# Unpacked expert weights, and their cast on GpSimd instead of ScalarE, in the last stage of a four-part transformer kernel

## The chip, the cores and the metric

The kernel runs on one core of a Trainium2 chip. The metric is the device time of one execution in microseconds. A core has the engines TensorE (PE), VectorE (DVE), ScalarE (ACT), GpSimd (POOL) and SyncE (SP), and 16 DMA engines that all queues share.

## The reference

x has 4 x 1024 tokens of 256 numbers. Four parts follow one another, each added to x after a layer norm:

```python
x = x + _L0_attn_ref(_layernorm(x), ...)   # a gated recurrence over the sequence
x = x + _L0_ffn_ref(_layernorm(x), ...)    # 8 experts, the 2 best of each token
x = x + _L1_attn_ref(_layernorm(x), ...)   # causal attention, 16 heads of 64
x = x + _L1_ffn_ref(_layernorm(x), ...)    # 32 experts, the 4 best of each token
```

The last part is the one that the change touches. D is 256, I is 128, E is 32, K is 4, and an expert takes at most C = 256 tokens. The expert weights W1, W3 (32 x 256 x 128) and W2 (32 x 128 x 256) are bfloat16:

```python
scores = jax.nn.sigmoid((X @ gate_w.T).astype(jnp.float32))
_, idx = jax.lax.top_k(scores + bias[None, :], K)
...
xe = jnp.zeros((E, C, D), x.dtype).at[eid, posc].add(jnp.where(valid[:, None], Xrep, ...))
h = jax.nn.silu(jnp.einsum('ecd,edi->eci', xe, W1)) * jnp.einsum('ecd,edi->eci', xe, W3)
ye = jnp.einsum('eci,eid->ecd', h, W2)
...
out = yrows.reshape(-1, K, D).sum(axis=1)
out = out + jax.nn.silu(X @ sw1.T) * (X @ sw3.T) @ sw2.T
```

## The kernel before

Each engine has its own program, in one block, and they meet through semaphores. Four stages stand one after another with a barrier between them (finish_stage). The first three (recurrence, first experts, attention) end at about 2093 us.

The fourth stage first finishes the routing of the last tokens and computes the shared expert for 8 groups of 512 tokens. POOL scatters each token's normalised row, with its token number and its gates, to the places that its experts have in the HBM tensor routed1 (scatter_rows, L856). Rows of it are 289 numbers, 1156 B.

Then come the 32 routed experts. For one expert e, which uses the slot q = e mod 8 (EBUF is 8) of each buffer:

- SP loads its 256 rows into d_xe (load_rows, L739) and its packed weights, 128 partitions x 768 bfloat16 numbers, into d_wb (load_weights, L733). The first eight experts' weights are loaded at the start of the stage, all others when VectorE and the casting engine are done with the slot (s_dec2, s_dec), after the rows of the same expert.
- A cast makes 32-bit numbers of them in d_wf. ScalarE casts W1 and W3 (128 x 512, cast_weights, L1254), four experts ahead; VectorE casts W2 (128 x 256, L1920).
- TensorE transposes the rows (transpose_rows, L2472) and ScalarE and VectorE split them in a high and a low part (L1227, L1904). VectorE also copies token numbers and gates out (d_tok, d_gate, L1902 and L1903), for which the slot's previous scatter must have landed.
- TensorE multiplies by W1 and W3 (hidden, L2485). ScalarE's tanh (L1231) and VectorE (L1912, L1914) make the gated hidden layer d_eh, which is again split (L1236, and L1924 for d_eh_lo).
- TensorE multiplies by W2 (second_layer, L2496), ScalarE scales by the gates into d_y (take_y, L1246). d_y has 4 slots (YBUF), so this waits until the rows of the expert four before have landed.
- POOL adds the 2 x 128 rows into one of two accumulators in HBM, acc[0] for even and acc[1] for odd experts, with an indirect DMA that adds (add_rows, L923). It waits for the tile of d_y and for the previous adds to the same accumulator.

TensorE runs hidden(e), transpose_rows(e + 2), second_layer(e - 2) in turn. When all adds have landed, SP loads both accumulators, 8 groups of 512 tokens each (L761), VectorE adds them (L1948), and ScalarE's queue stores the result (L1293). In these loads and stores, partition p has 4 neighbouring tokens of a group, 4096 B in one run.

Of the kernel before, what the change touches and what calls it, by code (L numbers as in the profile page):

```python
# [11 lines left out]
ACT = mybir.ActivationFunctionType  # L12
AX_X = mybir.AxisListType.X

P = 128
# [27 lines left out]
        self.eng.wait_ge(self.sem, at if self.i is None else self.i * self.per + at)  # L43


def network(nc, x_in, a_params, w12T, w3T, gate0T, wqkT, wvT, woT, swT, bias1, ewT, out):
    B, S, D = x_in.shape
    T = B * S
    NT = T // P
    KD = D // P  # L50
# [2 lines left out]
    K0 = 2  # L53
    NH, DQ = wqkT.shape[2], wqkT.shape[3] // 2
    N = (a_params.shape[1] - 3 * D - 4 - 2 * KD) // (4 * KD)
    E1, I1 = bias1.shape[0], ewT.shape[1]
    K1 = 4
    C1 = 2 * (2 * 512) * K1 // E1
    G = 4
    GT = G * P  # L60
    NG = T // GT
# [9 lines left out]
    Z_SCALE = (DQ / D) ** 0.5 * (D / DQ) ** 0.5 / NH  # L71

    x_tiles = x_in.rearrange("b (i p) d -> p (b i) d", p=P)
    out_rows = out.rearrange("b s d -> (b s) d")
    TOK, GATE = D, D + 1
    FIRST, GAP, SECOND = D + 1, D + 2, D + 3
    routed0 = nc.dram_tensor("routed0", (E0 * REGION, D + 4), F32).ap()
# [5 lines left out]
    routed1 = nc.dram_tensor("routed1", (E1 * C1, W_ROW), F32).ap()  # L83
# [3 lines left out]
    with ExitStack() as ctx:  # L87
# [42 lines left out]
        X = place("X", [P, NT, D])  # L130
# [164 lines left out]
        EBUF = 8  # L295
# [270 lines left out]
        def _(sp):  # L566
# [162 lines left out]
            def load_weights(e, q):  # L729

                sp.wait_ge(s_dec, e + 1)
                sp.wait_ge(s_dec2, e + 1)
                sp.dma_start(d_wb[:, q, :], ewT[bass.ds(e, 1), :, :].rearrange("e p d -> p (e d)")).then_inc(s_dw[q], 16)  # L733

            def load_rows(e, q):

                sp.wait_ge(s_det, e + 1)
                sp.wait_ge(s_dgt, e * 2 + 2)
                sp.dma_start(d_xe[:, q, :, :], routed1[bass.ds(e * C1, C1), :].rearrange("(p a) d -> p a d", p=P)).then_inc(s_dxe[q], 16)  # L739


            for q in range(EBUF):
# [16 lines left out]
            for g in range(NG):  # L759
                for j, rows in enumerate((X, d_acc)):  # L760
                    sp.dma_start(rows[:, g * G:(g + 1) * G, :],  # L761
                                 acc[j][g * GT:(g + 1) * GT, :].rearrange("(p q) d -> p q d", p=P)).then_inc(s_x[g], 16)
            sp.wait_ge(s_out, 16 * NG)

        @block.gpsimd
        def _(pool):
# [50 lines left out]
            def add_rows(n, r):  # L817

                if not (isinstance(n, int) and n == 0):
                    pool.wait_ge(s_bst, n * 16)  # L820
                pool.wait_ge(s_btk, n + 3)
                pool.wait_ge(s_bye, n + 3)
                pool.sem_inc(s_pass, 1)
                pool.indirect_dma_start(acc0, bass.IndirectOffsetOnAxis(ap=b_tok[:, r:r + 1], axis=0),  # L824
                                        b_y[:, r, :], None, compute_op=ALU.add).then_inc(s_bst, 16)
# [84 lines left out]
            for n in range(2):  # L910
                pool.wait_ge(s_dslot, NG - 1 + n)
                scatter_rows(NG - 2 + n, n, range(G * K1))

            def add_rows(e, half, q):

                j = q % 2

                if not (isinstance(half, int) and half == 0):
                    pool.wait_ge(s_dyst[j], half * 32)
                for a in range(C1 // P):  # L920
                    pool.wait_ge(s_dye, e * 2 + (a + 5))
                    pool.sem_inc(s_pass, 1)
                    pool.indirect_dma_start(acc[j], bass.IndirectOffsetOnAxis(ap=d_tok[:, q, a:a + 1], axis=0),  # L923
                                            d_y[:, q % YBUF, a, :], None, compute_op=ALU.add).then_inc(s_dyst[j], 16)

            pool.wait_ge(s_dax, 16 * (NT + 2 * (C1 // P) + NG))
            for q in range(EBUF):
                add_rows(q, q // 2, q)
            with pool.Fori(0, E1 // EBUF - 1) as i:
                for q in range(EBUF):  # L930
                    add_rows(i * EBUF + (q + EBUF), i * (EBUF // 2) + (EBUF // 2 + q // 2), q)

        @block.scalar
        def _(act):
# [311 lines left out]
                    act.activation(d_y[:, q % YBUF, a, :], PS[:, 4 + q % 2, a * D:(a + 1) * D], ACT.Identity,  # L1246
                                   bias=zeros[:, 0:1], scale=d_gate[:, q, a:a + 1]).then_inc(s_dye, 1)

            def cast_weights(e, q, eighth):

                act.wait_ge(s_dw[q], eighth * 16 + 16)

                act.wait_ge(s_deh, e + 1)
                act.activation(d_wf[:, q, 0:2 * D], d_wb[:, q, 0:2 * D], ACT.Copy).then_inc(s_dec, 1)  # L1254

            for c in range(4):
                cast_weights(c, c, 0)
            for j in range(2):
                take_rows(j, j)
            for e in range(2):  # L1260
                tanh_half(e, e)
                take_rows(e + 2, e)
                cast_weights(e + 4, e + 4, 0)
                take_hidden(e, e)

            for r in range(EBUF):
                tanh_half(r + 2, r % 2)
                take_rows(r + 4, r % 2)
                cast_weights(r + 6, (r + 6) % EBUF, (r + 6) // EBUF)
                take_y(r, r // 2, r, r >= YBUF)  # L1270
                take_hidden(r + 2, r % 2)
            with act.Fori(0, E1 // EBUF - 2) as i:
                for r in range(EBUF):
                    e, j = i * EBUF + (EBUF + r + 2), r % 2
                    tanh_half(e, j)
                    take_rows(e + 2, j)
                    cast_weights(e + 4, (r + 6) % EBUF, i + (1 + (r + 6) // EBUF))
                    take_y(e - 2, i * (EBUF // 2) + (EBUF // 2 + r // 2), r)
                    take_hidden(e, j)
            for r in range(EBUF - 2):  # L1280
                e, j = E1 - EBUF + r + 2, r % 2
                tanh_half(e, j)
                if e + 2 < E1:
                    take_rows(e + 2, j)
                if e + 4 < E1:
                    cast_weights(e + 4, (e + 4) % EBUF, E1 // EBUF - 1)
                take_y(e - 2, (e - 2) // 2, r)
                take_hidden(e, j)
            for e in range(E1 - 2, E1):
                take_y(e, e // 2, e % EBUF)  # L1290
            for g in range(NG):
                act.wait_ge(s_x4, g + 1)
                act.dma_start(out_rows[g * GT:(g + 1) * GT, :].rearrange("(p q) d -> p q d", p=P), X[:, g * G:(g + 1) * G, :]).then_inc(s_out, 16)  # L1293

        @block.vector
        def _(dve):
# [610 lines left out]
            def gate_hidden(e, q, eighth, ahead):  # L1907
                j = q % 2
                dve.wait_ge(s_deth, e + 1)

                dve.wait_ge(s_deg, e + 1)
                st.done(dve.scalar_tensor_tensor(d_eh[:, j, :], d_eth[:, j, :], 1.0, PS[:, 2 + j, 0:C1], ALU.add, ALU.mult))  # L1912
                st.sync()
                dve.scalar_tensor_tensor(d_eh[:, j, :], d_eh[:, j, :], 0.5, PS[:, 2 + j, C1:2 * C1], ALU.mult, ALU.mult).then_inc(s_dep, 1)  # L1914
                if ahead:
                    low_rows(e + 2, (q + 2) % EBUF, eighth * (EBUF // 2) + (q + 2) // 2, not isinstance(e, int) or e + 2 >= EBUF)
                dve.wait_ge(s_dw[q], eighth * 16 + 16)

                dve.wait_ge(s_dey, e + 1)
                dve.tensor_copy(d_wf[:, q, 2 * D:3 * D], d_wb[:, q, 2 * D:3 * D]).then_inc(s_dec2, 1)  # L1920
# [652 lines left out]
```

## Time and profile before

| | |
|---|---|
| median of 3 runs | 2332.34 us (2330.44 to 2339.95) |
| the profiled execution | 2332.34 us, of which the span is 2330.6 us |
| mean granted TensorE clock | 0.918 of full speed |
| last stage, first load to end | about 2093 to 2330.6 us |
| scatter-adds of the routed experts | 64, from 2172.34 to 2291.64 us (starts) |

The span is the time from the first to the last recorded instruction. The profile is of one execution. Times inside it are given in microseconds from the start of the span, or in nanoseconds for the mean of one instruction. The rest of the profile is in the section with rows.

### The profile page before, as it was taken

The page shows a single profiled execution, that of the slowest core. Times are in us where ns is not written, and L with a number is a line of the kernel's source. Part 1 is how long each engine was busy: PE and PEld are TensorE (multiplying, and loading weights), DVE is VectorE, ACT ScalarE, POOL GpSimd, SP SyncE. Part 2 cuts the span into 40 slices and gives each one's busy share as a digit, 9 for nine tenths or more (in the row PEclk, how much of TensorE's full clock was granted, in tenths as well). Part 3 has the DMA queues.
Part 4 walks back from the last instruction along what each step waited for, and adds up shares of the span by engine and source line. Part 5 has one row for each costly group of instructions (what it writes and reads, how often), then busy time and mean ns, then how long its engine had stood idle before and what let it go on. Part 6 is the DMA issues. An engine that isn't in the chain of part 4 may idle for free. (4 is left out here: it accounts for less than half of the span.)

```text
span 2330.6 us, 42176 instructions
## 1 busy us (share of the span) xinstructions
PE 2000.4 (86%) x11537; PEld 1412.2 (61%) x11538; DVE 1362.5 (58%) x3643; ACT 1024.4 (44%) x2148; POOL 1144.8 (49%) x1128
## 2 busy tenths in 40 slices
PE   4662999998957999989999989999989999966660
PEld 2352566665635777767777767777767777745550
DVE  7753333332335666665778765777765778648661
ACT  2210333332323555545555544555545555523660
POOL 0055222222210666643667753567753667745583
PEclk8855999999977999999999989999999999987995
DMA  8194222234250111111222111211111111113987
GB/s 309 65 294 166 49 45 45 45 59 131 45 142 18 45 47 46 46 36 33 57 66 55 48 28 32 61 53 48 45 29 42 47 53 47 43 39 126 225 146 244
DMA packets 203593, 186.44 MB, mean 80 GB/s; under 512 B 85418, under 2 KB 184583, under 8 KB 201872
## 3 DMA queue, kind: packets, MB, share of 16 engines
q1 hardware_dynamic: 173168, 149.15, 21.5%
q0 software_dynamic: 29088, 30.89, 8.2%
q10 hardware_dynamic: 1152, 4.19, 0.4%
q8 instruction: 85, 1.39, 0.2%
q14 instruction: 100, 0.82, 0.1%
HBM read 101.74 MB, written 82.95 MB: 79 GB/s over the span
## 5 line engine op out<-in xcount | busy, mean ns | idle before, releaser
L881 POOL TENSOR_TENSOR c_den<-c_den,c_p 128x512 f32<-128x512 f32 (+3 forms) x576 | 550.9, 956 | 359.5 <-ACT c_p L1094 288.5
L1094 ACT ACTIVATE c_p<-PS 128x512 f32<-128x512 f32 (+3 forms) x768 | 350.5, 487 | 348.7 <-PE PS L2178 236.6
L2199 PE MATMUL PS<-c_p,c_vh 128*64 128x256 f32 (+1 forms) x2816 | 336.1, 352 | 0.0
L2147 PE MATMUL PS<-c_k,c_q 128*128 128x512 f32 (+2 forms) x768 | 291.1, 381 | 29.8 <-DVE c_max L1601 20.4
L2170 PE MATMUL PS<-c_q,c_k 128*128 128x512 f32 (+2 forms) x768 | 293.0, 385 | 3.3 <-issue 2.2
L2049 PE MATMUL PS<-b_w12T,b_tT 128*128 x576 | 273.7, 598 | 1.4 <-ACT b_tT L988 0.7
L824 POOL DMA_INDIRECT acc<-b_y,b_tok x72 | 111.1, 1543 | 332.4 <-ACT b_y L1005 303.7
L2199 PEld LDWEIGHTS PS<-c_p,c_vh 128*64 128x64 f32 x2816 | 198.4, 137 | 107.0 <-issue 53.6
L2171 PE MATMUL PS<-c_q,c_k 128*128 128x512 f32 (+2 forms) x768 | 259.1, 348 | 0.0
L1085 ACT ACTIVATE c_q<-PS 64x512 fp32r<-64x512 f32 x256 | 151.2, 591 | 176.1 <-PE PS L2134 172.9
L1608 DVE CUSTOM_DVE_ANT_0 PS<-PS,c_maskq 128x128 f32<-128x128 f32 (+3 forms) x256 | 127.0, 501 | 144.9 <-PE PS L2147 138.1
L2147 PEld LDWEIGHTS PS<-c_k,c_q 128*128 128x128 f32 x768 | 147.8, 193 | 93.8 <-issue 28.9
L1608 DVE CUSTOM_DVE_ANT_0 PS<-PS,c_maskq,c_max 128x128 f32<-128x128 f32 (+3 forms) x256 | 143.1, 559 | 104.5 <-PE PS L2147 79.7
L1601 DVE TENSOR_REDUCE c_max<-PS 128x1 f32<-128x512 f32 x256 | 171.9, 672 | 54.8 <-PE PS L2147 54.5
L1509 DVE SCALAR_TENSOR_TENSOR b_hid<-b_sg,PS 128x512 f32<-128x512 f32 x72 | 49.5, 688 | 248.8 <-ACT b_sg L992 248.8
L2170 PEld LDWEIGHTS PS<-c_q,c_k 128*128 128x128 f32 x768 | 145.4, 189 | 65.5 <-issue 30.1
L856 POOL DMA_INDIRECT routed<-r_rows,r_slot x128 | 131.3, 1026 | 66.3 <-DVEq L1711 38.8
L2049 PEld LDWEIGHTS PS<-b_w12T,b_tT 128*128 128x128 f32 x576 | 104.9, 192 | 77.0 <-issue 73.3
L2171 PEld LDWEIGHTS PS<-c_q,c_k 128*128 128x128 f32 x768 | 146.0, 190 | 9.1
L2065 PE MATMUL PS<-b_w3T,b_hT 128*128 x576 | 138.3, 383 | 1.4 <-ACT b_hT L996 1.1
L2219 PE MATMUL PS<-c_wo,c_yT 128*128 128x256 f32 x512 | 129.4, 398 | 8.0 <-DVE c_yT L1620 8.0
L1628 DVE SCALAR_TENSOR_TENSOR X<-PS,X 128x512 f32<-128x512 f32 (+1 forms) x128 | 88.6, 692 | 64.8 <-PE PS L2219 64.8
(286 smaller groups left out, 3562.1 us busy)
## 6 DMA issues: line engine op xcount, KB each, us to landing
c_vh<-c_v SPq DMA_DIRECT2D x64, 256.0 KB
c_rrow<-rden SPq DMA_DIRECT2D x64, 256.0 KB, 3.5
b_xt<-routed SPq DMA_DIRECT2D x72, 130.0 KB, 2.1
routed<-b_empty SPq DMA_DIRECT2D x32, 289.0 KB
d_xe<-routed SPq DMA_DIRECT2D x32, 289.0 KB, 4.3
b_w12T<-in_w12T_dram SPq DMA_DIRECT2D x16, 512.0 KB, 13.4
acc<-X SPq DMA_DIRECT2D x16, 512.0 KB, 2.9
X<-acc SPq DMA_DIRECT2D x16, 512.0 KB, 10.1
```

The lines of the kernel that those rows point to most:

```text
L856: pool.indirect_dma_start(routed1, bass.IndirectOffsetOnAxis(ap=r_slot[n][:, j // K1, j % K1:j % K1 + 1], axis=0), r_rows[n][:, j // K1, : ...
L881: pool.tensor_tensor(c_den[c][:, off:], c_den[c][:, off:], p, ALU.add).then_inc(s_cPa, 1)
L1085: act.activation(dst, src, ACT.Copy).then_inc(s_cqs, 1)
L1094: act.activation(c_p[:, P_AT[m]:P_AT[m] + WIDTH[m]], PS[:, ST_BANK[m % ROUND], skip:skip + WIDTH[m]], ACT.Exp, scale=ATT_SCALE).then_inc(s ...
L1601: dve.tensor_reduce(dst, src, AX_X, ALU.max).then_inc(s_turn[bank], 1)
L1608: dve.tensor_tensor_reduce(src, src, c_maskq[:, 512 - w:512], 1.0, dst if c else BIG, ALU.add, ALU.max, dst).then_inc(s_turn[bank], 1)
L2049: ins = pe.matmul(PS[:, 2 * j + c, :], b_tT[:, j, k, :], b_w12T[:, k, bass.ds(e * (2 * H0) + c * H0, H0)], start=(k == 0), stop=(k == KD - 1))
L2065: ins = pe.matmul(PS[:, 6 + j, 0:D], b_hT[:, j, k, :], b_w3T[:, k, bass.ds(e * D, D)], start=(k == 0), stop=(k == KH - 1))
L2147: pe.matmul(PS[:, 2 + use[0], 0:max(w, 256)], c_q1[h][:, t * P:(t + 1) * P], c_k1[h][:, c * 512:c * 512 + max(w, 256)], start=True, stop=T ...
L2170: pe.matmul(PS[:, bank, 0:n], c_k1[h][:, j * P:(j + 1) * P], c_q1[h][:, q], start=True, stop=False)
L2171: ins = pe.matmul(PS[:, bank, 0:n], c_k2[h][:, j * P:(j + 1) * P], c_q2[h][:, q], start=False, stop=not diagonal)
L2199: ins = pe.matmul(dst, c_vh[h][:, j, :], moving, start=(j == 0), stop=(t0 == 2 + a))
```

## The change

The expert weights are no longer packed on the host. W1, W3 and W2 come as they are, and load_weights issues three DMAs for each expert. The runs in HBM that land in one partition are 256 B for W1 and W3 (two for each) and 512 B for W2. The semaphore of a slot counts 48 for each expert and not 16.

The cast of W1 and W3 goes from ScalarE to POOL, with the same shape. POOL's program has, for each expert c, cast_weights(c) and then, from c = 6 (LAG) on, add_rows(c - 6); the last six experts' adds follow without a cast. The wait for the accumulators' first contents, once ahead of all adds, comes after the seventh cast.

The rows of an expert, the two accumulators and the output are read and stored with partition p holding every 128th token: rows p and 128 + p of an expert, in runs of 1156 B where they were 2312 B, and 4 runs of 1024 B where there was one of 4096 B.

```diff
-                sp.dma_start(d_wb[:, q, :], ewT[bass.ds(e, 1), :, :].rearrange("e p d -> p (e d)")).then_inc(s_dw[q], 16)
+                for n, w in enumerate((W1, W3)):
+                    sp.dma_start(d_wb[:, q, n * D:(n + 1) * D].rearrange("p (k i) -> p k i", k=KD),
+                                 w[bass.ds(e, 1), :, :].rearrange("e (k p) i -> p (e k) i", p=P)).then_inc(s_dw[q], 16)
+                sp.dma_start(d_wb[:, q, 2 * D:3 * D], W2[bass.ds(e, 1), :, :].rearrange("e i d -> i (e d)")).then_inc(s_dw[q], 16)
...
-                sp.dma_start(d_xe[:, q, :, :], routed1[bass.ds(e * C1, C1), :].rearrange("(p a) d -> p a d", p=P)).then_inc(s_dxe[q], 16)
+                sp.dma_start(d_xe[:, q, :, :], routed1[bass.ds(e * C1, C1), :].rearrange("(a p) d -> p a d", p=P)).then_inc(s_dxe[q], 16)
...
-                                 acc[j][g * GT:(g + 1) * GT, :].rearrange("(p q) d -> p q d", p=P)).then_inc(s_x[g], 16)
+                                 acc[j][g * GT:(g + 1) * GT, :].rearrange("(q p) d -> p q d", p=P)).then_inc(s_x[g], 16)
...
+            def cast_weights(e, q, eighth):
+
+                pool.wait_ge(s_dw[q], eighth * 48 + 48)
+
+                pool.wait_ge(s_deh, e + 1)
+                pool.sem_inc(s_pass, 1)
+                pool.tensor_copy(d_wf[:, q, 0:2 * D], d_wb[:, q, 0:2 * D]).then_inc(s_dec, 1)
...
-            pool.wait_ge(s_dax, 16 * (NT + 2 * (C1 // P) + NG))
-            for q in range(EBUF):
-                add_rows(q, q // 2, q)
+            LAG = 6
+            for c in range(EBUF):
+                cast_weights(c, c, 0)
+                if c == LAG:
+                    pool.wait_ge(s_dax, 16 * (NT + 2 * (C1 // P) + NG))
+                if c >= LAG:
+                    add_rows(c - LAG, (c - LAG) // 2, c - LAG)
             with pool.Fori(0, E1 // EBUF - 1) as i:
                 for q in range(EBUF):
-                    add_rows(i * EBUF + (q + EBUF), i * (EBUF // 2) + (EBUF // 2 + q // 2), q)
+                    cast_weights(i * EBUF + (EBUF + q), q, i + 1)
+                    e = EBUF + q - LAG
+                    add_rows(i * EBUF + e, i * (EBUF // 2) + e // 2, e % EBUF)
+            for e in range(E1 - LAG, E1):
+                add_rows(e, e // 2, e % EBUF)
...
-            def cast_weights(e, q, eighth):
-
-                act.wait_ge(s_dw[q], eighth * 16 + 16)
-
-                act.wait_ge(s_deh, e + 1)
-                act.activation(d_wf[:, q, 0:2 * D], d_wb[:, q, 0:2 * D], ACT.Copy).then_inc(s_dec, 1)
...
-                act.dma_start(out_rows[g * GT:(g + 1) * GT, :].rearrange("(p q) d -> p q d", p=P), X[:, g * G:(g + 1) * G, :]).then_inc(s_out, 16)
+                act.dma_start(out_tiles[:, g * G:(g + 1) * G, :], X[:, g * G:(g + 1) * G, :]).then_inc(s_out, 16)
...
-                dve.wait_ge(s_dw[q], eighth * 16 + 16)
+                dve.wait_ge(s_dw[q], eighth * 48 + 48)
```

ScalarE's calls of cast_weights go too (the first four experts ahead of its loop, then one in each round).

## Rows read from the trace of the kernel before

**Rows 1.** The page: engines' busy time, and the queue of SP's DMAs.

```profile
PE 2000.4 (86%) x11537; PEld 1412.2 (61%) x11538; DVE 1362.5 (58%) x3643; ACT 1024.4 (44%) x2148; POOL 1144.8 (49%) x1128
...
q1 hardware_dynamic: 173168, 149.15, 21.5%
```

**Rows 2.** Windows: length, busy time of PE, PEld, DVE, ACT, POOL, clock, DMA share, GB/s.

```profile
688.00:696.00 8.00, 4.65 (x17) 3.49 (x16) 5.01 (x11) 2.32 (x4) 0.00 (x0) 0.50 1.09 351
2306.00:2322.00 16.00, 0.00 (x0) 0.00 (x0) 4.89 (x4) 0.00 (x0) 0.00 (x0) 0.50 1.03 419
...
2184.73:2241.35 56.62, 34.72 (x240) 30.73 (x240) 34.80 (x108) 40.16 (x94) 47.02 (x31) 0.94 1.00 202
2248.92:2289.79 40.87, 16.41 (x100) 14.10 (x100) 14.51 (x44) 16.80 (x39) 34.17 (x23) 0.74 0.62 71
```

**Rows 3.** Groups by line from 2090 us on: busy us, mean ns, idle before.

```profile
L923 POOL DMA_INDIRECT acc<-d_y,d_tok x64 | 99.9, 1562 | 39.9 <-ACT d_y L1246 24.6 <-issue 13.4 <-DMA acc<-d_y,d_tok 1.9
...
L1254 ACT ACTIVATE d_wf<-d_wb 128x512 fp32r<-128x512 bf16 x32 | 20.5, 648 | 0.0
```

**Rows 4.** Timeline of POOL, last stage: start, duration, what, idle before it.

```profile
2152.39 0.98 POOL L856 DMA_INDIRECT routed<-r_rows,r_slot  x1 [0.30 <-issue]
2172.34 1.58 POOL L923 DMA_INDIRECT acc<-d_y,d_tok  x1 [18.97 <-ACT d_y L1246]
...
2184.73 1.55 POOL L923 DMA_INDIRECT acc<-d_y,d_tok  x1 [0.73 <-ACT d_y L1246]
...
2241.35 1.55 POOL L923 DMA_INDIRECT acc<-d_y,d_tok  x1 [0.30 <-issue]
...
2248.92 1.55 POOL L923 DMA_INDIRECT acc<-d_y,d_tok  x1 [0.30 <-issue]
...
2291.64 1.56 POOL L923 DMA_INDIRECT acc<-d_y,d_tok  x1 [0.30 <-issue]
```

**Rows 5.** Timeline of ScalarE before the first output tile.

```profile
2166.47 0.62 ACT L1254 ACTIVATE d_wf<-d_wb 128x512 fp32r<-128x512 bf16 x1
...
2170.96 1.02 ACT L1246 ACTIVATE d_y<-PS,zeros,d_gate 128x256 f32<-128x256 f32 x2 [0.50 <-DVE d_tok L1902]
```

**Rows 6.** Groups by line of POOL, whole span: its cast from bf16.

```profile
L901 POOL CAST r_s1T<-r_swb 128x512 fp32r<-128x512 bf16 x1 | 0.6, 607 | 0.0
```

**Rows 7.** Timeline of POOL in the attention stage.

```profile
1200.03 0.73 POOL L881 TENSOR_TENSOR c_den<-c_den,c_p 128x256 f32<-128x256 f32 x1 [0.18 <-POOL c_den L881]
1201.00 1.05 POOL L856 DMA_INDIRECT routed<-r_rows,r_slot  x1 [0.24 <-POOL c_den L881]
1202.07 0.47 POOL L881 TENSOR_TENSOR c_den<-c_den,c_p 128x128 f32<-128x128 f32 x1
...
1204.91 1.03 POOL L856 DMA_INDIRECT routed<-r_rows,r_slot  x1 [0.16 <-issue]
```

**Rows 8.** Timelines of VectorE and POOL, attention stage, near 1482 us.

```profile
1481.94 1.23 DVE L1620 TENSOR_TENSOR c_yT<-c_yT,c_rrow 128x1024 f32<-128x1024 f32 x1
...
1482.04 1.72 POOL L881 TENSOR_TENSOR c_den<-c_den,c_p 128x256 f32<-128x256 f32 x1 [0.18 <-POOL c_den L881]
```

**Rows 9.** DMA queues, 2184.73 to 2241.35: packets, MB, share of 16 engines.

```profile
q0 software_dynamic: 4288, 3.91, 52.1%
q1 hardware_dynamic: 4390, 7.50, 47.1%
```

**Rows 10.** DMA rate in 40 slices, 787.7 to 788.4: c_vh alone, 256 B runs.

```profile
GB/s 0 0 0 0 0 44 88 117 117 132 249 234 190 234 219 219 219 190 234 205 234 219 234 219 190 205 234 176 190 219 205 219 205 205 219 219 219 205 190 205
```

**Rows 11.** Timeline of SP's queue: the first eight experts' weights.

```profile
2096.10 4.48 SPq L733 DMA_DIRECT2D d_wb<-in_ewT_dram  x8
```

**Rows 12.** What SP's queue waited for from 2090 us on: us, times, longest.

```profile
SPq L732 <- DVE d_wf L1920: 53.0, 24, 4.8
```

**Rows 13.** The chain that ended last: start, us, what.

```profile
2302.68 23.56 DMA d_acc<-acc
2326.26 1.23 DVE X L1948
```

More of the change, by code:

```diff
@@ L43, in sync, with network @@
         self.eng.wait_ge(self.sem, at if self.i is None else self.i * self.per + at)
-def network(nc, x_in, a_params, w12T, w3T, gate0T, wqkT, wvT, woT, swT, bias1, ewT, out):
+def network(nc, x_in, a_params, w12T, w3T, gate0T, wqkT, wvT, woT, swT, bias1, W1, W3, W2, out):
     B, S, D = x_in.shape
@@ L55, in network @@
     N = (a_params.shape[1] - 3 * D - 4 - 2 * KD) // (4 * KD)
-    E1, I1 = bias1.shape[0], ewT.shape[1]
+    E1, _, I1 = W1.shape
     K1 = 4
@@ L73, in network @@
     x_tiles = x_in.rearrange("b (i p) d -> p (b i) d", p=P)
-    out_rows = out.rearrange("b s d -> (b s) d")
+    out_tiles = out.rearrange("b (i p) d -> p (b i) d", p=P)
     TOK, GATE = D, D + 1
@@ L1247, in take_y @@
                                    bias=zeros[:, 0:1], scale=d_gate[:, q, a:a + 1]).then_inc(s_dye, 1)
-            def cast_weights(e, q, eighth):
-                act.wait_ge(s_dw[q], eighth * 16 + 16)
-                act.wait_ge(s_deh, e + 1)
-                act.activation(d_wf[:, q, 0:2 * D], d_wb[:, q, 0:2 * D], ACT.Copy).then_inc(s_dec, 1)
-            for c in range(4):
-                cast_weights(c, c, 0)
             for j in range(2):
@@ L1262, in _ @@
                 take_rows(e + 2, e)
-                cast_weights(e + 4, e + 4, 0)
                 take_hidden(e, e)
@@ L1268, in _ @@
                 take_rows(r + 4, r % 2)
-                cast_weights(r + 6, (r + 6) % EBUF, (r + 6) // EBUF)
                 take_y(r, r // 2, r, r >= YBUF)
@@ L1276, in _ @@
                     take_rows(e + 2, j)
-                    cast_weights(e + 4, (r + 6) % EBUF, i + (1 + (r + 6) // EBUF))
                     take_y(e - 2, i * (EBUF // 2) + (EBUF // 2 + r // 2), r)
@@ L1284, in _ @@
                     take_rows(e + 2, j)
-                if e + 4 < E1:
-                    cast_weights(e + 4, (e + 4) % EBUF, E1 // EBUF - 1)
                 take_y(e - 2, (e - 2) // 2, r)
@@ L2556 @@
         'swT': _np.concatenate([flat(rows(gate1.T)), flat(rows(_np.stack([sw1.T, sw3.T], axis=1))), sw2.T], axis=1),
-        'bias1': bias1, 'ewT': _np.concatenate([w.reshape(w.shape[0], w.shape[1] // P, P, -1).swapaxes(1, 2).reshape(w.shape[0], P, -1)
-                                                for w in (W1, W3, W2)], axis=2),
+        'bias1': bias1, 'W1': W1, 'W3': W3, 'W2': W2,
     }
```

## The prediction

> **What bounds the kernel now.** The page's busy times come first [rows 1]: TensorE is busy for 86% of the span, GpSimd (POOL) for only 49%. That is an average over four stages, and the change touches none of the first three, so I read only the last one, the routed experts of layer 1, from about 2093 us on.
>
> In that stage the table of windows [rows 2] has three parts with different limits. From 2184.73 to 2241.35 TensorE, VectorE and ScalarE are busy 61 to 71% of the time, POOL 83%, and the DMA engines' share is 1.00. From 2248.92 to 2289.79 the DMA share falls to 0.62, the others sink further, and POOL still has 34.17 of 40.87 us. From 2306 to 2322 nothing computes except a few adds, and DMA is full.
>
> Which of POOL and DMA paces the loop is decided by POOL's own timeline [rows 4]. Its scatter-adds (two for each expert, 64 in all) start at 2184.73 and, 30 starts later, at 2241.35: 1.887 us each. From 2248.92 to 2291.64 it is 23 steps of 1.857 us. So the spacing stays the same when the DMA share drops by 0.38: POOL paces both parts, with 1.56 us for one instruction [rows 3] and 0.30 us of "issue" between two. An expert costs POOL 2 x 1.86 = 3.72 us. The grouped row agrees: 39.9 us idle before these instructions, of which 19.0 is the one wait before the first, and the other 20.9 is nearly all the 0.30 gap. DMA is a close second: at share 1.00 it is just keeping up.
>
> The tail follows: the last scatter starts at 2291.64, SyncE (SP) then issues 16 loads, and the chain shows 23.56 us of DMA up to the last add at 2326.26 [rows 13].
>
> **The change part by part.**
>
> *The cast of W1 and W3 moves from ScalarE to POOL.* ScalarE loses 32 casts of 0.648 us [rows 3]. It isn't the limit in the loop, so most of that buys nothing. Ahead of the first output tile (2170.96) it does three of them between other work, and the first begins at 2166.47 [rows 5]: at most 3 x 0.648 = 1.9 us. Not all lies on the path (some is hidden by TensorE), so I take 1.0 us gained, bounds 0 and 1.9.
>
> POOL gains 32 casts of 128x512 from bf16. The trace has one such instruction on POOL, 607 ns [rows 6]. What stands around it: after a POOL arithmetic instruction the next indirect DMA starts 0.24 us later, and the arithmetic after an indirect DMA 0.02 us later [rows 7], against 0.30 between two indirect DMAs. So a cast put between two scatters adds 0.607 + 0.02 + 0.24 - 0.30 = 0.57 us. Bounds from the same rows: 0.49 (the next such gap is 0.16) to 0.91 (the whole 0.30 stays, before and after).
>
> How many of the 32 are on the path: POOL is free from 2153.4, when its last routing scatter ends, to 2172.34 [rows 4]. Casts 0 to 6 stand ahead of the first scatter-add in program order: 7 x 0.8 = 5.6 us inside 18.9 us of idleness, free. They are done by about 2159, when the first y tile is still 12 us off [rows 5]. Without that cover they would cost 5.6 us. The other 25 (experts 7 to 31) stand between scatter-adds. Their inputs aren't late: the weights of an expert are fetched eight experts ahead, and POOL casts only six ahead of its own adds. What is queued behind a waiting cast is the next scatter-add, and behind that the release of d_y and d_tok; since POOL now loses only 2.0 us beyond its fixed gaps, what it waits for is in time, and it will ask for it later than now. So I expect no new wait there. 25 x 0.57 = 14.3 us.
>
> *POOL and VectorE get in each other's way.* Where VectorE runs a tensor_tensor with both inputs in SBUF (1.23 us at 1481.94), a POOL 128x256 add that starts 0.1 us later lasts 1.72 us [rows 8] and not 0.73 [rows 7]: it is held until the other ends. In the expert loop VectorE has one instruction of this kind for each expert, d_eh_lo with 0.42 us. An arrival at random within 4.3 us would meet it about one time in four and lose 0.2 us: 0.05 us. As both are driven by the same landings, I double it: 0.1 us for each cast, 25 x 0.1 = 2.5 us, bounds 0 and 0.42 x 25 = 10.5. The Trainium skill (SBUF — State Buffer, "Who interferes with whom") has this as a rule: a VectorE instruction with two SBUF inputs and a GpSimd instruction that reads SBUF exclude each other for the whole instruction. The trace agrees, with the 1.72 us above. ScalarE, by that page, never waits on anyone, so the rule speaks against this move.
>
> *The weights arrive in three DMAs of short runs.* Each expert's one load (128 runs of 1536 B) becomes W1 and W3 with 256 runs of 256 B each and W2 with 128 of 512 B: 640 packets for 128. *The rows of an expert* come as 256 runs of 1156 B, not 128 of 2312 B. Prices: runs of 256 B move at about 210 GB/s (SBUF to SBUF, the nearest row) [rows 10]; about 1 KB at 351, 4 KB at 419 [rows 2]. Alone, the present 0.492 MB of an expert takes about 1.25 us at 395 GB/s; (my value for 1.5 to 2.3 KB, between 351 and 419); afterwards 0.131/210 + 0.066/260 + 0.296/351 = 0.62 + 0.25 + 0.84 = 1.71 us (260 for 512 B, between its neighbours), a factor of 1.37. In the loop, 15 experts take 56.62 us, 3.77 us each; q1 has 47.1% of the engines, 1.78 us, and the scatters' q0 52.1%, 1.97 us [rows 9]. Afterwards 1.78 x 1.37 + 1.97 = 4.41 us. POOL afterwards: 3.72 + 0.57 + 0.1 = 4.39. The two tie, and two saturated servers delay each other: I add 0.1 us for each of the 20 experts that go by while loads are still running, 2.0 us (bounds 0 and the DMA rival below).
>
> SP's issues: eight loads take 4.48 us at the stage's start [rows 11], 24 would take about 13.4 us, from 2096 to 2110, and the first weights are wanted at 2153, when POOL comes free: nothing. In the loop SP mostly waits for VectorE's cast of W2 (53.0 us in 24 waits [rows 12]); two more issues of 0.56 us fit into a mean wait of 2.2. The load of the next expert's rows stands behind them, eight experts ahead of need.
>
> *The end.* The 16 loads of 512 KB and the 8 stores go from runs of 4096 B to 1024 B. 12.58 MB at 419 GB/s are 30.0 us, at 351 GB/s 35.8: +5.8 us, all on the path, since DMA is full here. If only the loads (8.39 MB) slow down it is +3.9; the high bound is 8.
>
> **The sum.** 14.3 + 2.5 + 2.0 + 5.8 - 1.0 = 23.6 us. The profiled execution took 2332.34 us (span 2330.6 and 1.7 around it), which is also the median. Forecast: 2332.3 + 23.6 = 2356 us, 1.0% slower. What this kernel's measurement can tell from no change is 0.5%, or 11.7 us.
>
> **Rivals.**
>
> *A: DMA becomes the bound.* If short packets cost more in the mix than alone, q1 is the limit. Price them by the whole run: q1's 173168 packets took 21.5% of 16 engines, 46 ns each [rows 1]. 640 x 46 + 256 x 70 (between 46 and the 97 ns that q1's packets now take in the loop, 0.471 x 16 x 56.62 us / 4390) = 47.4 us over 16 engines is 2.96 us, with 1.97 for the scatters 4.93 us for an expert: 0.54 above the forecast's, for 20 experts +10.8, so 2365 us with the 2.0 of the sum replaced. For it speaks the share of 1.00 now; against it, that 256 B runs took only 19 ns (256 B at 210/16 GB/s). The Trainium skill (DMA: Bandwidth & Descriptors, "Specifications") asks for at least 512 B for full rate, and exempts SBUF to SBUF in "Why small descriptors are slow (HBM only)". The weights come from HBM, and no row here has 256 B runs from there, which is why this rival keeps some weight. Chance 0.20.
>
> *B: the casts are cheap and the port blocks nothing.* 25 x 0.50 = 12.5, end +3.9, start -1.9, nothing else: +14.5, 2347 us. Chance 0.20.
>
> *C: not slower.* POOL's arithmetic would have to run beside its descriptor work, so that casts fill the recorded 1.56 us instead of following it. Then only the end and the start are left: 5.8 - 1.0 = +4.8, 2337 us, within 0.5%. It decides if under 0.25 us of each cast shows on POOL (25 x 0.25 + 4.8 = 11.1). Against it: arithmetic and indirect DMAs follow one another without overlap in [rows 7]. Chance 0.04. To be faster by 0.5% it would take 12 us more at the start, where ScalarE can give 1.9: 0.02.
>
> *D: the port lock locks in phase.* VectorE's d_eh_lo meets every cast at its start: 10.5 in place of 2.5, 2364 us. Chance 0.12. The page on SBUF named above would allow it: whichever starts first keeps the port for its whole length.
>
> The forecast itself has 0.42. Cases from 2345 to 2368 hold 8 in 10 with the bounds above. The low edge of B reaches under the 11.7 us. Slower by over 0.5%: 0.92, within: 0.06, faster: 0.02.
>
> **What would show it.** Step by step in the changed kernel: POOL's cast at 0.6 to 0.75 us, 25 of them after the first scatter-add, and starts of the second adds of neighbouring experts 4.3 to 4.5 us apart, where they now are 3.72. In the last part, without loads and for experts with a cast, 4.3 to 4.4; the last six experts 3.72 again, as no cast is left. From first to last scatter start 119.3 us now, about 137 then. If rival A holds, the early loop is slower (4.9) than the late one, POOL waits for y or for a landing, and landings go beyond 6 us. From the last scatter's start to the span's end, 39 us now, about 45. The prediction is wrong if POOL shows new waits over a few us, or if the end doesn't grow.

## The result, and the profile after

The changed kernel takes 2350.81 us (median of 5 runs, 2348.84 to 2358.49) against 2333.24 us for the kernel before (5 runs, 2330.44 to 2339.95): 17.6 us more, a ratio of 1.0077 with a 95% interval of 1.0055 to 1.0098. The forecast was 2356 us (+23.6), with a range of 2345 to 2368. Five further executions of the changed kernel took 2345.97 to 2358.96 us. Of the experiments below, e4 has two of ten executions at 2553 and 6476 us, in a slow state, which are left out of its time.

The span grew from 2330.6 to 2348.7 us, by 18.1. It splits at three marks that both traces have:

| stretch | before, us | after, us | growth |
|---|---|---|---|
| start of the span to the first load of the last stage | 2093.11 | 2093.43 | 0.3 |
| from there to the first scatter-add | 79.23 | 81.22 | 2.0 |
| first to last start of the 64 scatter-adds ("the loop") | 119.30 | 132.40 | 13.1 |
| last start to the span's end ("the end") | 38.96 | 41.65 | 2.7 |

First the groups by line from 2090 us on, which answer to [rows 3] (busy us, mean ns, then idle time before them and what ended it):

```profile
L934 POOL DMA_INDIRECT acc<-d_y,d_tok x64 | 99.8, 1559 | 31.2 <-ACT d_y L1265 15.8 <-issue 12.2 <-DMA acc<-d_y,d_tok 2.7
...
L923 POOL CAST d_wf<-d_wb 128x512 fp32r<-128x512 bf16 x32 | 36.5, 1156 | 0.0
```

The scatter-adds last as long as before. The cast is recorded with 1156 ns, nearly twice what a POOL cast took in [rows 6]. POOL's timeline tells what that record holds (start, duration, what, idle before); it answers to [rows 4]:

```profile
2155.42 3.96 POOL L923 CAST d_wf<-d_wb 128x512 fp32r<-128x512 bf16 x7
2174.65 1.58 POOL L934 DMA_INDIRECT acc<-d_y,d_tok  x1 [15.27 <-ACT d_y L1265]
...
2196.14 1.56 POOL L934 DMA_INDIRECT acc<-d_y,d_tok  x1 [0.17 <-issue]
2198.00 1.56 POOL L934 DMA_INDIRECT acc<-d_y,d_tok  x1 [0.30 <-issue]
2198.98 1.20 POOL L923 CAST d_wf<-d_wb 128x512 fp32r<-128x512 bf16 x1
2200.36 1.56 POOL L934 DMA_INDIRECT acc<-d_y,d_tok  x1 [0.17 <-issue]
...
2236.97 1.56 POOL L934 DMA_INDIRECT acc<-d_y,d_tok  x1 [0.31 <-DMA acc<-d_y,d_tok]
2237.96 1.35 POOL L923 CAST d_wf<-d_wb 128x512 fp32r<-128x512 bf16 x1
2239.48 1.56 POOL L934 DMA_INDIRECT acc<-d_y,d_tok  x1 [0.17 <-issue]
...
2307.05 1.55 POOL L934 DMA_INDIRECT acc<-d_y,d_tok  x1 [0.30 <-issue]
```

Seven casts in a row take 3.96 us, 0.57 each. Behind a scatter-add the record of a cast begins 0.58 us before that scatter-add ends (2198.98 against 2198.00 + 1.56), so 1.20 us of record are 0.62 us of work behind it. What counts is the step from one scatter-add to the next: 2.36 us with a 1.20 us cast between (2198.00 to 2200.36), 2.51 us with a 1.35 us cast (2236.97 to 2239.48), 1.86 without. A cast costs 0.50 or 0.65 us. Of the 25 casts behind the first scatter-add, 8 have 1.20 to 1.22 us and 17 have 1.30 to 1.42.

Two pieces of VectorE's timeline show the difference, the first away from any POOL cast (the one before it has ended at 2195.97), the second beside the cast at 2237.96:

```profile
2196.18 0.42 DVE L1929 TENSOR_TENSOR d_eh_lo<-d_eh,d_eh_hi 128x256 fp32r<-128x256 f32 x1
...
2237.69 0.43 DVE L1925 CAST d_wf<-d_wb 128x256 fp32r<-128x256 bf16 x1
2238.04 0.82 DVE L1929 TENSOR_TENSOR d_eh_lo<-d_eh,d_eh_hi 128x256 fp32r<-128x256 f32 x1
```

The subtraction at 2196.18 has no cast beside it and takes 0.42 us. The one at 2238.04 begins 0.49 us before the scatter-add ahead of the cast ends (2238.53), takes 0.82 us itself, and the cast is 0.15 us longer. The same holds for 15 of the 17 long casts: each has a subtraction of 0.82 or 0.83 us that begins 0.44 to 0.50 us before that end. The other two (1.30 and 1.31 us) begin their work together with VectorE's cast of W2. None of the eight short ones meets a subtraction.

The windows, which answer to [rows 2] (length, busy time of PE, PEld, DVE, ACT, POOL, clock, DMA share, GB/s), and the queues of the same stretch as in [rows 9]:

```profile
2184.73:2241.35 56.62, 34.65 (x227) 30.47 (x225) 37.00 (x95) 28.96 (x70) 50.03 (x41) 0.91 0.99 190
2263.19:2284.77 21.58, 13.91 (x77) 12.17 (x76) 14.45 (x35) 9.81 (x24) 19.19 (x16) 0.74 0.54 62
2316.00:2322.00 6.00, 0.00 (x0) 0.00 (x0) 2.45 (x2) 0.00 (x0) 0.00 (x0) 0.50 1.10 348
2326.00:2340.00 14.00, 0.00 (x0) 0.00 (x0) 3.68 (x3) 0.00 (x0) 0.00 (x0) 0.50 1.09 382
```

```profile
q1 hardware_dynamic: 14226, 7.22, 51.4%
q0 software_dynamic: 3863, 3.52, 47.7%
```

The DMA share in the loop is 0.99, as it was 1.00, though q1 moves 3.2 times as many packets (14226 for 4390). So that share told little of how much room was left. At the end the 1 KB runs go at 348 GB/s while loads are alone and at 382 with stores beside them, where the kernel before, with 4 KB runs, had 419 for loads and stores together (2306 to 2322).

### The profile page after: what moved, and what is told of

Read it like the earlier page. It is cut to its first block and busy times, and to the rows that moved or that the text cites. A ratio compares the mean times of both kernels' runs of the same rounds, so it can differ in the third digit from the quotient of the medians.

```text
span 2348.7 us, 42315 instructions
## 1 busy us (share of the span) xinstructions
PE 2008.2 (86%) x11537; PEld 1419.8 (60%) x11538; DVE 1377.0 (59%) x3643; ACT 1007.6 (43%) x2116; POOL 1166.8 (50%) x1160
## 3 DMA queue, kind: packets, MB, share of 16 engines
q1 hardware_dynamic: 200816, 149.15, 21.9%
```

## The experiments

None of the eleven ran on the chip of the two profiles above; they ran on three others (e1 to e4, e5 to e8, and e9 to e11 share one each). The kernel before takes 2378 to 2380 us on each of these, and each ratio is against runs of it on the same chip. The times that the expectations of e1 to e4 name are those of the first chip, so only their differences count. The single times of e6, e8, e9 and e11 say nothing of their edits: the stretch from POOL's last routing scatter to its first scatter-add has nearly the same work in all kernels, and varies there from 29.6 us (e6) to 43.8 us (e11), for 19.0 and 19.2 in the first two profiles. The loop and the end do not contain it. The stretches are read from each kernel's own trace; "excess" is what the records of the casts behind the first scatter-add have over 1.20 us, in sum.

| kernel | time, us | ratio (95%) | loop, us | end, us | long casts of 25, excess us |
|---|---|---|---|---|---|
| e9_before_again | 2382.48 | one run | 121.95 | 39.30 | none |
| e10_after_again | 2394.69 | 1.0066 (1.0043 to 1.0090) | 132.83 | 41.27 | 18, 2.7 |
| e1_cast_on_scalar | 2382.82 | 1.0023 (1.0006 to 1.0041) | 121.84 | 41.74 | none |
| e2_cast_on_pool_only | 2392.50 | 1.0063 (1.0040 to 1.0085) | 132.75 | 38.99 | 18, 2.7 |
| e7_short_runs_only | 2378.53 | 1.0001 (0.9980 to 1.0022) | 121.68 | 38.92 | none |
| e3_end_runs_only | 2383.16 | 1.0012 (0.9992 to 1.0032) | 122.35 | 41.99 | none |
| e8_loads_short_stores_long | 2380.91 | one run | 120.68 | 41.56 | none |
| e4_no_shared_reads | 2392.68 | 1.0053 (1.0029 to 1.0078) | 130.42 | 41.71 | 7, 0.8 |
| e5_w2_on_scalar | 2391.80 | 1.0059 (1.0035 to 1.0082) | 132.42 | 41.64 | 8, 1.7 |
| e6_no_vector_port | 2382.50 | one run | 129.59 | 41.54 | 0, 0.1 |
| e11_cast_split | 2402.01 | one run | 133.90 | 41.60 | pairs of 1.32 to 1.67, not comparable |

**The two kernels again (e9, e10).** No edits.

> The kernel before once more, for its stages on the chip of these runs. Theory: the loop 119 to 123 us, the end 39.0 us, from the stage's first load to the end of POOL's last routing scatter 60 to 61 us; what else is longer than in the first profile lies outside the stage's loop and end.

> The changed kernel once more. Theory (the 2 us later start was TensorE's clock at the logits, not the change): the loop 132 to 133 us, the end 41.7 us, and the stretch from the first load of the stage to the end of the last routing scatter within the spread of the other kernels, 60.3 to 62.3 us, with no tie to the way the weights are loaded. Rival (24 weight loads for 8 delay the loads of d_xT or the routing): 62 us again, and 60 to 61 in the kernels with packed loads. Ratio to before 1.006 to 1.008.

The loops differ by 10.9 us and the ends by 2.0; the ratio is 1.0066. From the stage's first load to the end of POOL's last routing scatter they take 59.4 and 61.0 us (60.3 and 62.0 on the first chip); e9's lies just below what was expected. What the "later start" is, is told with e7 below.

**The cast alone, and everything but the cast (e1, e2).** e1 takes the changed kernel and puts cast_weights back in ScalarE's program:

```diff
-                pool.tensor_copy(d_wf[:, q, 0:2 * D], d_wb[:, q, 0:2 * D]).then_inc(s_dec, 1)
+                act.activation(d_wf[:, q, 0:2 * D], d_wb[:, q, 0:2 * D], ACT.Copy).then_inc(s_dec, 1)
```

> The changed kernel, but with the cast of W1 and W3 back on ScalarE, as before; the three short-run weight loads, the 1156 B rows and the 1 KB runs at the end stay. Theory (POOL's own work paces the expert loop, the cast costs 13 us there, the end 2.7 us): the loop from first to last scatter-add returns to 119 to 121 us, the end stays at 41.6 us from the last scatter-add's start, the time is 2336 to 2339 us. Rival (the short runs make DMA the bound, and the cast only looks guilty): the loop stays above 125 us and the time above 2343 us.

e2 is the reverse: the kernel before, with POOL's cast and its order of casts and adds, and the packed loads.

> The kernel before with nothing changed but the cast of W1 and W3, which moves to POOL in the order of the changed kernel; all transfers as before. Theory: the loop takes 132 us from first to last scatter-add as in the changed kernel, the end stays at 39.0 us, the time is 2346 to 2348 us. Rival (part of the loop's growth came from short runs and the late landings they cause): the loop takes 128 us or less. If the later start by 2 us in the changed kernel belongs to TensorE's clock and not to the cast, it may or may not be there here.

The loop follows the cast and nothing else: 121.84 us with all the short runs and no cast on POOL, 132.75 with packed loads and the cast. With the cast on POOL the short runs add nothing that shows (e10's loop is 132.83 us, e2's 132.75). The rival that the short runs make the loop long falls with both. e1's loop, away from the early experts, is back at the spacing of [rows 4]:

```profile
2299.88 1.55 POOL L926 DMA_INDIRECT acc<-d_y,d_tok  x1 [0.30 <-issue]
2301.73 1.56 POOL L926 DMA_INDIRECT acc<-d_y,d_tok  x1 [0.30 <-DMA acc<-d_y,d_tok]
2303.59 1.55 POOL L926 DMA_INDIRECT acc<-d_y,d_tok  x1 [0.30 <-issue]
```

**The short runs alone (e7).** The kernel before with the changed load_weights and load_rows:

```diff
-                sp.dma_start(d_wb[:, q, :], ewT[bass.ds(e, 1), :, :].rearrange("e p d -> p (e d)")).then_inc(s_dw[q], 16)
+                for n, w in enumerate((W1, W3)):
+                    sp.dma_start(d_wb[:, q, n * D:(n + 1) * D].rearrange("p (k i) -> p k i", k=KD),
+                                 w[bass.ds(e, 1), :, :].rearrange("e (k p) i -> p (e k) i", p=P)).then_inc(s_dw[q], 16)
+                sp.dma_start(d_wb[:, q, 2 * D:3 * D], W2[bass.ds(e, 1), :, :].rearrange("e i d -> i (e d)")).then_inc(s_dw[q], 16)
...
-                sp.dma_start(d_xe[:, q, :, :], routed1[bass.ds(e * C1, C1), :].rearrange("(p a) d -> p a d", p=P)).then_inc(s_dxe[q], 16)
+                sp.dma_start(d_xe[:, q, :, :], routed1[bass.ds(e * C1, C1), :].rearrange("(a p) d -> p a d", p=P)).then_inc(s_dxe[q], 16)
```

> The kernel before with nothing changed but three short-run loads of each expert's weights (256 B and 512 B) and 1156 B runs for its rows; casts and the end as before. Theory (DMA has room in the loop, POOL paces it): the loop 119 to 123 us as in the kernel before, the end 39.0 us, the time within 2 us of before. Rival, the prediction's price for DMA (4.41 us of DMA for each expert with loads): the first 20 experts take 88 us where they take 75, the loop 130 us and more, the time 2391.

A ratio of 1.0001, a loop of 121.68 us for e9's 121.95. The loops of the kernels with ScalarE's cast and packed loads lie between 120.68 (e8) and 122.35 us (e3), so their spread is 1.7 us. e7's queues from 2225 to 2280 us, in the middle of the loop (packets, MB, share):

```profile
q1 hardware_dynamic: 14384, 7.35, 55.3%
q0 software_dynamic: 4051, 3.69, 45.0%
```

That is the pace of [rows 9] (7.35 MB in 55 us, 7.50 MB in 56.62 us) with 3.3 times the packets. By the prediction's 4.41 us of DMA for an expert, in place of 3.77, the loop would be some 13 us longer (20 x 0.64). So the short runs cost nothing that shows, though q1 and q0 together are at a share of 1.00 here too.

The stretch ahead of the first scatter-add is settled by one pair of windows, from 5 to 10 us after the stage's first load, while TensorE makes the last logits. Here are the kernel before, the changed kernel, e3 (loads as before) and e7 (short loads), in this order:

```profile
2098.11:2103.11 5.00, 3.98 (x33) 3.85 (x31) 2.66 (x19) 1.30 (x2) 0.00 (x0) 0.79 1.02 408
```

```profile
2098.43:2103.43 5.00, 5.00 (x26) 5.00 (x24) 0.98 (x7) 1.30 (x2) 0.00 (x0) 0.50 1.05 390
```

```profile
2125.03:2130.03 5.00, 5.00 (x26) 5.00 (x24) 0.99 (x7) 1.30 (x2) 0.00 (x0) 0.50 1.02 406
```

```profile
2122.80:2127.80 5.00, 3.99 (x32) 3.86 (x31) 2.67 (x19) 1.30 (x2) 0.00 (x0) 0.79 1.04 395
```

The mean granted clock is either 0.50, the lower level of 1.2 GHz all through, or 0.78 to 0.82, where the step up to 2.4 GHz falls inside. With it VectorE's wait for ScalarE's tanh of those logits is 6.0 us, or 4.2 to 4.3, and nothing between occurs. Of the 13 profiles five have 6.0: the changed kernel twice, e1, e4, and e3, whose transfers up to there are those of the kernel before. The eight with 4.2 are the kernel before twice, e2, e5, e6, e7, e8 and e11; of these e5, e6, e7 and e11 load the short runs. So 1.8 of the 2.0 us belong to this two-valued start, and it does not follow from the way in which weights are loaded. Whether short loads make the later value likelier (four of eight profiles have it, one of five with packed loads) is not shown; nor is what sets it.

**The end (e3, e8).** e3 is the kernel before with 1 KB runs in the last loads and stores, e8 with 1 KB runs in the loads alone (its stores still put 4 neighbouring rows in a partition, so rows of the result come in another order within a group):

```diff
-                                 acc[j][g * GT:(g + 1) * GT, :].rearrange("(p q) d -> p q d", p=P)).then_inc(s_x[g], 16)
+                                 acc[j][g * GT:(g + 1) * GT, :].rearrange("(q p) d -> p q d", p=P)).then_inc(s_x[g], 16)
```

> The kernel before with nothing changed but the runs of 1024 B in the last loads and stores. Theory: from the last scatter-add's start to the span's end 41.6 us for 39.0, loads alone at 348 GB/s and loads with stores at 385 GB/s (now 420), the loop unchanged; the time 2335 to 2337 us, against before +2.7. Rival, the price in the prediction (351 GB/s all through): +5.8 us, 2338 to 2339. Rival two (the end in the changed kernel grew for another reason, the place of the last landings): no change.

> The kernel before, but only the last 16 loads have runs of 1024 B; the stores keep 4096 B, so the result's rows come in another order within a group. Theory (loads with 1 KB runs go at 348 GB/s while alone, and short runs cost less when loads and stores run together): from the last scatter-add's start to the end 41 to 41.7 us, so nearly the whole growth of the end (38.96 to 41.65) comes from the loads. Rival (loads and stores share it by their bytes, 2 to 1): 40.7 to 40.8 us.

The end is 41.99 us in e3 and 41.56 in e8, where kernels with 4 KB runs have 38.92 to 39.30 and those with 1 KB runs 41.27 to 41.99. The time of e3 alone would not have told it (1.0012, with 1 inside the interval). e3's rates in 40 slices of its last 38 us:

```profile
GB/s 1 37 123 338 386 365 347 346 349 349 350 346 352 388 383 385 387 384 386 385 385 385 387 365 373 386 384 384 373 389 386 381 385 387 381 384 194 0 254 298
```

and e8's:

```profile
GB/s 0 56 207 382 378 347 346 352 346 349 349 369 397 383 400 420 361 389 414 367 367 347 346 367 416 376 364 369 398 389 369 348 391 401 418 395 22 69 410 73
```

Loads alone run at some 348 GB/s in both. Later e8 swings between 347 (loads alone again) and 420 (a 4 KB store beside them), and e3 stays at 385. The two ends differ by 0.4 us, less than the 0.7 by which those with 1 KB runs differ among themselves: the stores' run length costs nothing that shows, the loads' costs it all.

**Who holds up POOL's cast (e4, e5, e6).** e4 is the changed kernel with an instruction that reads nothing in the place of VectorE's subtraction (the low half of the hidden layer is zero):

```diff
-                dve.tensor_tensor(d_ehs[1][:, j, :], d_eh[:, j, :], d_ehs[0][:, j, :].bitcast(F32), ALU.subtract).then_inc(s_deg, 1)
+                dve.memset(d_ehs[1][:, j, :].bitcast(F32), 0.0).then_inc(s_deg, 1)
```

> The changed kernel, but VectorE fills the low half of the hidden layer (d_eh_lo) with zeros by a memset, which reads nothing from SBUF; so the subtraction of two SBUF tiles is left out, and the result has lower precision. Theory (the 1.35 us casts are those that meet this subtraction, the 1.20 us ones don't): all casts show 1.20 us, the step of an expert is 4.22 us for 4.37, the loop is 2 to 3 us shorter, the time about 2348 us. Rival (the long casts meet VectorE's cast of W2 or another instruction): still two kinds of casts and no gain.

All casts of 1.35 us are gone, but seven of 1.29 or 1.30 us stay, so the theory was half right: another instruction blocks too. e5 keeps the subtraction and takes the cast of W2 off VectorE:

```diff
-                dve.tensor_copy(d_wf[:, q, 2 * D:3 * D], d_wb[:, q, 2 * D:3 * D]).then_inc(s_dec2, 1)
+                act.activation(d_wf[:, q, 2 * D:3 * D], d_wb[:, q, 2 * D:3 * D], ACT.Copy).then_inc(s_dec2, 1)
```

> The changed kernel, but the cast of W2 leaves VectorE and takes the place on ScalarE that the cast of W1 and W3 had before. VectorE then has one instruction in the expert loop that shuts POOL out, d_eh_lo, and no cast. Theory (both VectorE's cast and d_eh_lo hold the port, and either can delay POOL's cast): fewer long casts, the loop 131 to 132.5 us, at most 1 us off. Rival (VectorE's cast reads one tile and doesn't matter): the same share of 1.35 us casts (some 14 of 25) and an unchanged loop of 132.4 to 132.8.

Fewer casts are long (8 of 25), but up to 1.45 us, and the scatter-adds are 0.9 us longer in sum than in the changed kernel's first profile (0.5 in e10); the loop of 132.42 us lies in the theory's range and in the rival's. The share of long casts is not the rival's, but alone this run decides little. e6 has both edits:

> e5_w2_on_scalar with the low half of the hidden layer filled with zeros by a memset too (the subtraction of two SBUF tiles is left out). VectorE then has neither a cast nor an instruction with two SBUF inputs beside POOL's casts, only copies of two columns. Theory: all 25 casts of 1.19 to 1.23 us, the step of an expert 4.22 us with hardly any spread, the loop 129.0 to 130.0 us. Rival (the 1.30 us casts that were left without the subtraction come from POOL's own side): still some of 1.30 us.

Every cast takes 1.20 to 1.22 us now, and from the second expert on the steps are 4.21 to 4.23 us as long as there are casts. A piece of POOL's timeline in e6:

```profile
2270.53 1.56 POOL L934 DMA_INDIRECT acc<-d_y,d_tok  x1 [0.30 <-issue]
2271.52 1.20 POOL L923 CAST d_wf<-d_wb 128x512 fp32r<-128x512 bf16 x1
2272.89 1.56 POOL L934 DMA_INDIRECT acc<-d_y,d_tok  x1 [0.17 <-issue]
2274.75 1.56 POOL L934 DMA_INDIRECT acc<-d_y,d_tok  x1 [0.30 <-issue]
2275.74 1.20 POOL L923 CAST d_wf<-d_wb 128x512 fp32r<-128x512 bf16 x1
```

The loop is 129.59 us for 132.83, 3.2 us less. Of this 2.6 are the casts' excess (2.7 us in e10, 0.1 here); the other 0.6 are scatter-adds that are shorter in sum (99.7 us for 100.3), which is within what that sum varies by among the 13 profiles (99.7 to 100.8). Of the excess, the subtraction's removal alone takes 1.9 us (e4).

The traces also show who holds whom, and from when. Two casts of POOL in e4, each with the scatter-add before it and VectorE's cast of W2:

```profile
2226.86 1.56 POOL L934 DMA_INDIRECT acc<-d_y,d_tok  x1 [0.30 <-issue]
2227.85 1.30 POOL L923 CAST d_wf<-d_wb 128x512 fp32r<-128x512 bf16 x1
2228.42 0.28 DVE L1925 CAST d_wf<-d_wb 128x256 fp32r<-128x256 bf16 x1
...
2235.51 1.56 POOL L934 DMA_INDIRECT acc<-d_y,d_tok  x1 [0.30 <-issue]
2236.50 1.20 POOL L923 CAST d_wf<-d_wb 128x512 fp32r<-128x512 bf16 x1
2237.14 0.72 DVE L1925 CAST d_wf<-d_wb 128x256 fp32r<-128x256 bf16 x1
```

Started just as the scatter-add ends (2228.42), VectorE's cast takes its usual 0.28 us and POOL's waits; started 0.07 us behind that end (2237.07), it takes 0.72 us and POOL's has its 1.20. And a subtraction that begins 0.49 us before a scatter-add ends takes 0.41 us where no POOL cast stands behind, as here in e7, and 0.82 where one does:

```profile
2308.36 1.56 POOL L926 DMA_INDIRECT acc<-d_y,d_tok  x1 [0.31 <-DMA acc<-d_y,d_tok]
2309.43 0.41 DVE L1927 TENSOR_TENSOR d_eh_lo<-d_eh,d_eh_hi 128x256 fp32r<-128x256 f32 x1
```

So the cast holds VectorE up before the scatter-add ahead of it has ended. What the cast loses itself is what VectorE's instruction lasts beyond 0.18 us behind the scatter-add's end: 0.15 us for an end at 0.33 us (the subtractions that begin 0.49 us before), 0.10 for 0.28 (W2's cast, above), 0.23 to 0.25 for 0.41 (e5).

**A cast in two pieces (e11).** The changed kernel with two instructions of 128x256, and the counts of s_dec doubled:

```diff
-                pool.tensor_copy(d_wf[:, q, 0:2 * D], d_wb[:, q, 0:2 * D]).then_inc(s_dec, 1)
+                for n in range(2):
+                    pool.tensor_copy(d_wf[:, q, n * D:(n + 1) * D], d_wb[:, q, n * D:(n + 1) * D]).then_inc(s_dec, 1)
```

> The changed kernel, but the cast of W1 and W3 is two instructions of 128x256 on POOL, not one of 128x512. It tells how much of a cast's 0.50 us in the loop is fixed. Theory (0.50 us are the columns' 0.6 us less a gap that is hidden; the one 128x256 cast in the trace of before took 0.397 us for 0.607): an expert's step grows by 0.15 to 0.25 us over 4.22 to 4.37, the loop is 136 to 138.5 us. Rival (the fixed part is hidden under the scatter's own work): less than 0.05 us, the loop 132 to 133.5 us.

Neither: the step is mostly 4.34 us, 0.12 over 4.22, and the loop 133.90, 1.1 over e10. The unhindered pair takes 1.32 us where one takes 1.20. One more instruction costs 0.12 us; if the first costs as much, which this run can't separate, most of the 0.50 us is the columns.

None of these kernels is faster than the kernel before. What the loop leaves to gain is in the 64 scatter-adds, which neither kernel touches. The version that keeps the unpacked weights for nothing is e7.

## Why the prediction was right, point by point

**What paces the loop.** Right, for the reason given: e2 and e1 move the loop by 10.9 us with the cast alone. But "POOL paces both parts" was not the whole of it. The kernel before loses some time on POOL in the early loop: 1.8 us above its fixed gaps, of which this is the longest, between the fourth and the fifth scatter-add:

```profile
2180.58 1.55 POOL L923 DMA_INDIRECT acc<-d_y,d_tok  x1 [1.01 <-DMA acc<-d_y,d_tok]
```

In e9 such waits come to 4.4 us. No kernel with casts on POOL has any such wait above 0.31 us. The slower POOL no longer catches up with what it waits for.

The whole growth of the span, 18.1 us, is 12.5 (25 casts at 0.50), 2.6 (VectorE in their way), -2.0 (mostly these waits), 2.0 (the start), 2.7 (the end) and 0.3 before the stage. The forecast of 23.6 was 6 us too high, its loop alone by 5.7. Of its signs, the steps came out at 4.21 to 4.43 us for 4.3 to 4.5, the loop at 132.4 us for about 137, and the end at 41.65 for about 45; neither of the two signs of being wrong came. The cast's record was to be 0.6 to 0.75 us and is 1.20 to 1.42, because it overlaps the scatter-add's.

**The term "25 x 0.57 = 14.3".** The count of 25 was right. The price was 0.50 us for an unhindered cast, the prediction's lower bound: 12.5 us. The step that was a little off is the gap between a cast and the next indirect DMA, 0.17 us and not 0.24 [rows 7].

**The port, "25 x 0.1 = 2.5".** Measured 2.6 us in the changed kernel's profile (sum of the excess over 1.20 us), and e6 shows the cause (2.7 in e10, 0.1 without the two instructions). That the size came out is luck: the prediction took one cast in four to meet VectorE, at 0.2 us, and doubled the product by a guess. Measured are 17 of 25, at 0.15 us. They meet in phase, at the same offset of 0.49 us in most, as rival D had it, but for a third of its price. The prediction named d_eh_lo only; VectorE's cast of W2 does it as well. The rule of the Trainium skill that the prediction cited (SBUF — State Buffer, "Who interferes with whom") names casts too, among what can take the shared pair. e4 to e6 agree: seven casts are still 0.1 us longer when only the subtraction is gone, and none when both are.

**Short runs in the loop, "I add 0.1 us for each of the 20 experts, 2.0 us".** Wrong, in the term and in how it was priced. e7 shows nothing, with 14384 packets in q1 in 55 us where [rows 9] have 4390 in 56.62 us. The failed step is "q1 has 47.1% of the engines, 1.78 us", scaled by the ratio of times alone. That share is no price of these bytes: with 3.3 times the packets at the same pace it is 55.3% in e7, and q0's falls from 52.1 to 45.0% (51.4 and 47.7% in the changed kernel). So part of what was taken for work must have been waiting. Rival A (DMA as the bound, 2365 us) falls with it. 14.3 + 2.5 + 2.0 = 18.8 was forecast for the loop. The profile has 13.1, and 12.5 + 2.6 for the casts leave -2.0 in the place of this term, near the 1.8 us of waits that the kernel before has and the changed one has not. For e9 and e10 it is 12.5 + 2.7 - 4.4 = 10.8, and 10.9 is measured.

**The start, "-1.0".** Not confirmed. Between the end of POOL's last routing scatter and its first scatter-add there are 19.0 us before and 19.2 after, so taking ScalarE's casts away gained nothing there. The 2.0 us later start goes for 1.8 us with the clock's two-valued start, as 13 profiles show. The prediction had no term for it.

**The end, "+5.8, all on the path".** The direction was right, the size was 2.7 us. The mis-sized step is the rate: 351 GB/s was taken for all 12.58 MB, but it holds only while loads are alone. With stores beside them the rate is 382, and the kernel before did not have 419 all through either (342 GB/s from 2304 to 2308 us). "If only the loads slow down it is +3.9" had the right place, as e8 shows, with a price again too high.

**SP's issues, the free casts, the weights' lead.** As predicted. Seven casts ran in 3.96 us from 2155.42 on, 15 us before the first scatter-add, and no wait for weights shows in the loop.

**Rivals.** C (not slower) needed under 0.25 us for a cast on POOL; the least is 0.50. D (all casts meet the port, +10.5) falls in its price: a meeting costs 0.10 to 0.22 us. B was nearest in its cast price (0.50), though it denied the port, and its 2347 us are a little nearer to the measured 2350.8 than the forecast's 2356. The time alone does not tell the two apart; the 0.15 us that long casts take more, and e6, do.

## What to carry to other kernels

Before work moves to an engine, look at the spacing of what that engine does in the stretch that sets the end, not at its share of the span: POOL was busy for 49% of the span and had nothing to spare for 120 us. The price is then the number of moved instructions inside that spacing times what one adds to it, plus what a neighbour on a shared port costs, less the small waits that a slower engine no longer meets. And a DMA share of 1.00 doesn't say that there is no room: test it with more packets before pricing it.

## What the runs showed of the hardware that was not expected

- POOL's record of a cast that follows an indirect DMA overlaps that DMA's record by 0.58 us. Summing the records of the 25 casts in the loop (32.6 us) counts more than twice what they cost (12.5 + 2.6 = 15.1 us).
- In e7, 14384 packets in 55 us went through q1 at the same pace of the loop as 4390 in 56.62 us in the kernel before, with the DMA share at 1.00 both times.
- A POOL cast and VectorE's subtraction of two SBUF tiles that meet hold each other up on both sides: 0.82 us for 0.42 there, 1.35 for 1.20 here. With VectorE's cast the one that waits changes within 0.07 us of its start (e4: 1.30 for 1.20 us on POOL, or 0.72 for 0.28 on VectorE). And POOL's cast has its hold before the scatter-add ahead of it ends.
- On the chips of the experiments the profile books waits as "remote" that the first chip's profiles don't have, for instance in e3 (who waited: us, times, longest):

```profile
DVE b_tmp L1439 <- remote: 42.2, 6, 7.4
```

Such waits stand in all eleven profiles, in two places. The one above, with 3.1 us of waiting for TensorE beside it, is 45.3 us where the first chip's kernel before waits for TensorE for 21.9, and the last stage begins 22 to 29 us later. The other is in the shared expert of the last stage (VectorE's X, 7.6 to 19.6 us), where the stretch ahead of the first scatter-add is 11 to 25 us longer. Together they come near the 46 us that those chips take more for the kernel before (2379.5 for 2333.2). What stands behind them wasn't tried.
